# Windowed attention stream: keys, queries and values as one run at a slot's end, norms behind the products with V, the other engines reordered

## What is computed

```python
for i in range(DEPTH):
    x = attn_layer(shift_tokens(x), Wqkv[i], q_scale[i], k_scale[i], Wo[i]) + x
    x = ffn_layer(shift_tokens(x), ln_g[i], ln_b[i], W1[i], b1[i], W2[i], b2[i]) + x
```

## Time and profile before

| | us |
|---|---|
| median of three runs | 1957.38 |
| the profiled execution | 1957.33 |
| its span, first to last instruction | 1955.5 |
| TensorE busy | 1858.1 |
| VectorE busy | 1581.6 |
| ScalarE busy | 1405.1 |
| GpSimd busy | 1365.6 |

### The profile page before, as it was taken

The page is one execution under the profiler, slowest core; times in us unless marked ns, Lnnn a source line. Parts: engine busy times, 40 slices in busy tenths (PEclk is TensorE's granted clock), DMA queues, the critical chain, the costliest instruction groups (busy, mean ns, idle before and its releaser), DMA issues.

```text
span 1955.5 us, 68747 instructions
## 1 busy us (share of the span) xinstructions
PE 1858.1 (95%) x27097; PEld 1396.7 (71%) x27097; DVE 1581.6 (81%) x3046; ACT 1405.1 (72%) x2837; POOL 1365.6 (70%) x1442
## 2 busy tenths in 40 slices
PE   4999998899999999999999999999999999999998
PEld 3777766677777777777777777777777776777774
DVE  4677677898888888888888888888888888888876
ACT  2666665578777777777877777777777777777784
POOL 3000023798898787897878987878987879878780
PEclk9999999999999999999999999999999999999999
DMA  4000000344433334333334343443333343434332
GB/s 133 1 2 0 0 0 21 87 108 103 132 89 98 102 96 131 95 90 102 101 99 128 86 105 96 103 126 93 93 102 99 100 130 83 106 97 104 95 94 72
DMA packets 190582, 171.20 MB, mean 88 GB/s; under 512 B 32160, under 2 KB 186440, under 8 KB 190152
## 3 DMA queue, kind: packets, MB, share of 16 engines
q1 hardware_dynamic: 190280, 167.02, 32.6%
HBM read 21.14 MB, written 1.05 MB: 11 GB/s over the span
## 4 chain that ended last, share of the span: by engine, by line
PE 71%; ACT 12%; issue 7%; DVE 5%; POOL 2%; SPq 2%; DMA 1%; ACTq 0%; POOLq 0%; DVEq 0%
PE bank L896 7%; PE bank L934 7%; PE bank L864 7%; PE pair_bank L912 6%; PE bank L943 5%; PE bank L922 3%; PE bank L995 3%; PE bank L944 3%; PE bank L945 3%; PE bank L1017 3%; ACT sq L576 2%; PE bank L781 2%; PE bank L1009 2%; ACT probs L645 2%; PE pair_bank L903 2%
## 5 line engine op out<-in xcount | busy, mean ns | idle before, releaser
L415 POOL TENSOR_TENSOR z_raw<-rot_u,rot_v 128x256 f32<-128x256 f32 x768 | 553.6, 745 | 101.0 <-DVE rot_v L1210 94.4
L408 POOL TENSOR_TENSOR z_norm<-probs_t,z_raw 128x512 f32<-128x512 f32 x376 | 482.6, 1283 | 90.0 <-DVE probs_t L1289 87.3
L1209 DVE TENSOR_TENSOR rot_u<-bank,tabs 128x512 f32<-128x512 f32 x384 | 262.8, 684 | 166.6 <-ACT sq L576 166.3
L435 POOL TENSOR_TENSOR sqs<-sq 128x512 f32<-128x512 f32 x192 | 246.3, 1283 | 91.0 <-issue 90.8
L943 PE MATMUL bank<-x_high,w_high 128*128 128x256 f32 x768 | 301.4, 392 | 0.2 <-issue 0.2
L641 ACT ACTIVATE pair_bank<-pair_bank 128x512 f32<-128x512 f32 x192 | 111.7, 582 | 219.4 <-DVE pair_bank L1190 219.2
L576 ACT ACTIVATE sq<-bank 128x512 f32<-128x512 f32 x384 | 225.5, 589 | 49.6 <-PE bank L945 43.4
L1210 DVE TENSOR_TENSOR rot_v<-bank,tabs 128x512 f32<-128x512 f32 x384 | 261.0, 680 | 0.0
L934 PEld LDWEIGHTS bank<-probs_t,v_late 128*64 128x64 f32 x3072 | 155.0, 137 | 144.5 <-issue 144.5
L585 ACT ACTIVATE probs_t<-bank 64x512 f32<-64x512 f32 x384 | 226.8, 591 | 35.6 <-PE bank L922 33.3
L896 PE MATMUL bank<-sqs,consts 128*128 128x512 f32 x384 | 198.7, 599 | 25.2 <-POOL sqs L435 25.2
(11 more groups left out here) (186 smaller groups left out, 4545.7 us busy)
## 6 DMA issues: line engine op xcount, KB each, us to landing
zqk<-z_norm SPq DMA_DIRECT2D x1536, 64.0 KB, 2.1
v_late<-v_sb SPq DMA_DIRECT2D x192, 192.0 KB, 2.6
w_qkv<-in_L_ffn_Wqkv SPq DMA_DIRECT2D x18, 512.0 KB
v_late<-v_sb SPq DMA_DIRECT2D x192, 32.0 KB, 2.7
wo<-in_L_ffn_Wo SPq DMA_DIRECT2D x24, 128.0 KB, 2.4
w<-in_L_ffn_W SPq DMA_DIRECT2D x12, 170.5 KB, 2.9
consts<-in_constants SPq DMA_DIRECT2D x1, 1088.0 KB, 5.1
w_qkv<-in_L_attn_w_kv_up SPq DMA_DIRECT2D x2, 512.0 KB, 6.2
```

The costliest lines, as they stand in the source:

```text
L408: return pool.tensor_tensor(z_norm[:, parity, idx, :, :], rinv(m)[:, idx, :].unsqueeze(1).broadcast_to([P, 2, T]), z_raw[:, parity, idx, : ...
L415: a = pool.tensor_tensor(z_raw[:, parity, idx, half, :], rot_u[:, idx, half, :], rot_v[:, idx, 1 - half, :], ALU.add)
L1209: dve.tensor_tensor(rot_u[:, idx, :, :], src, tabs[:, 2 * idx, :, :], ALU.mult)
```

## The change

Only the order of steps within a slot moves, on four engines. The diff:

```diff
--- before.py
+++ after.py
@@ -420,8 +420,6 @@
                 if s == 0:
                     pool.wait_ge(S["pv_done"], STEPS)
                     pool.memset(spread[:, :, :, :], 0.0).then_inc(S["spread_zero"], 1)
-                if one:
-                    rotated(s + 4, s % 2, 1, "k_prod", "k_summed")
                 if two:
 
                     pool.wait_ge(S["bound_ready"], s + 4)
@@ -437,6 +435,7 @@
                     pool.wait_ge(S["q_summed"], s + 4)
                     normalise(s + 3, 0).then_inc(S["zn_ready"], 1)
                 if one:
+                    rotated(s + 4, s % 2, 1, "k_prod", "k_summed")
                     rotated(s + 4, s % 2, 0, "q_prod", "q_summed")
                 for g in range(G):
                     l = layer_begun(s, LAYER - 7 + g)
@@ -626,12 +625,12 @@
                 one, two = active(s, -4, GROUPS - 4), active(s, -3, GROUPS - 3)
                 three, four = active(s, 0, GROUPS), active(s, 1, GROUPS + 1)
                 normed = g == 0 and active(s, 2 * G, 2 * G + GROUPS)
-                if two and s >= 0:
-                    values_out(s + 3)
                 if s == 1:
                     act.wait_ge(S["spread_zero"], 2)
                 if four:
                     spread_out(s - 1)
+                if two and s >= 0:
+                    values_out(s + 3)
                 if mlp_slot(s, 17):
                     act.preload_act_table_set(LN_EXP)
                 if normed:
@@ -639,6 +638,8 @@
                 if three:
                     act.wait_ge(S["shifted"], s + 1)
                     act.activation(both, both, ACT.Exp).then_inc(S["raised"], 1)
+                if four:
+                    output_out(s - 1)
                 if two:
                     m = s + 3
                     act.wait_ge(S["n_done"], m + 1)
@@ -646,12 +647,6 @@
                     act.wait_ge(S["ln_done"], m + 1)
                     after(act, "zn_ready", m)
                     act.activation(rinv(m), ln_n(m), ACT.Exp, scale=-0.5).then_inc(S["rinv_ready"], 1)
-                if one:
-                    squares(s + 4, "k_prod", B_K, 1, "k_square")
-                l = layer_begun(s, LAYER - 5)
-                if l:
-                    rotary_scales(l)
-                    rotary_tables(l, 1)
                 l = layer_begun(s, LAYER - 4)
                 if l:
                     act.wait_ge(S["q_prod"], LAYER * l)
@@ -660,8 +655,6 @@
                     xc_squares((s - 7) // G)
                 if normed:
                     gained((s - 8) // G)
-                if four:
-                    output_out(s - 1)
                 for c in range(3):
                     if mlp_slot(s, 13 + c):
                         p = (s - 13 - c) // (2 * G)
@@ -673,8 +666,13 @@
                     gelus((s - 16) // (2 * G))
                 if one:
                     squares(s + 4, "lq_done", B_Q, 0, "q_square")
+                    squares(s + 4, "k_prod", B_K, 1, "k_square")
                 if session:
                     last_gelus((s - 16) // (2 * G))
+                l = layer_begun(s, LAYER - 5)
+                if l:
+                    rotary_scales(l)
+                    rotary_tables(l, 1)
                 l = layer_begun(s, LAYER + 6)
                 if l:
                     gains(l)
@@ -967,17 +965,15 @@
                     turn_windows(s - 1)
                 if active(s, 0, GROUPS):
                     windows(s, s // G, g)
-                if one:
-                    keys(s + 4)
                 if s == 0:
                     pe.wait_ge(S["yt_ready"], STEPS)
                     project_out(B_Y)
                 if active(s, 2, GROUPS + 2):
                     project_group(s - 2)
+                if four:
+                    weigh_windows(s - 1, (s - 1) // G, (s - 1) % G, (s - 1) // G % 2)
                 if two:
                     norms(s + 3)
-                if four:
-                    weigh_windows(s - 1, (s - 1) // G, (s - 1) % G, (s - 1) // G % 2)
                 for c in range(3):
                     if mlp_slot(s, 13 + c):
                         p = (s - 13 - c) // (2 * G)
@@ -1017,8 +1013,8 @@
                         mm = pe.matmul(B_M[:, :], w2[0:CW[c], c, :], hid[0:CW[c], c, :], start=(c == 0), stop=(c == 2))
                     mm.then_inc(S["mlp_done"], 1)
                 if one:
+                    keys(s + 4)
                     queries(s + 4)
-                if one:
                     values(s + 4, g, (s + 4) // G % 2)
                 if g == 2 and active(s, 6, 6 + GROUPS):
                     w, b = (s - 6) // G, (s - 6) // G % NB
@@ -1272,21 +1268,16 @@
             def slot(s):
                 g = s % G
                 one, two, three = active(s, -4, GROUPS - 4), active(s, -3, GROUPS - 3), active(s, 0, GROUPS)
+                if three:
+                    shift_windows(s)
                 if mlp_slot(s, 21):
                     mlp_residual((s - 21) // (2 * G), B_M)
                 if g == 3 and active(s, 7, 7 + GROUPS):
                     centred_out((s - 7) // G)
-                if three:
-                    shift_windows(s)
-                if one:
-                    rotate(s + 4, 1, B_K, "lk_done", "k_summed", "k_prod")
                 if g == 0 and active(s, 8, 8 + GROUPS):
                     normed_out((s - 8) // G)
                 if three:
                     weigh_down(s)
-                if two:
-                    dve.wait_ge(S["rinv_ready"], s + 4)
-                    dve.tensor_scalar(rinv(s + 3), rinv(s + 3), 1e12 / ROOT, None, ALU.min).then_inc(S["bound_ready"], 1)
                 if s == 0:
                     dve.wait_ge(S["wo_done"], NB + 1)
                     dve.tensor_copy(attn[:, NB - 1, :], B_Y[:, 0:T]).then_inc(S["res_done"], 1)
@@ -1301,7 +1292,11 @@
                     if mlp_slot(s, 17 + c):
                         p = (s - 17 - c) // (2 * G)
                         hidden_out(p, c, B_M, 2 * p + (2 if c == 2 else 1))
+                if two:
+                    dve.wait_ge(S["rinv_ready"], s + 4)
+                    dve.tensor_scalar(rinv(s + 3), rinv(s + 3), 1e12 / ROOT, None, ALU.min).then_inc(S["bound_ready"], 1)
                 if one:
+                    rotate(s + 4, 1, B_K, "lk_done", "k_summed", "k_prod")
                     rotate(s + 4, 0, B_Q, "q_square", "q_summed", "q_prod")
                 l = layer_begun(s, LAYER + 15)
                 if l:
```

## The result

| | us |
|---|---|
| before, median of 4 runs | 1957.74 (1956.3 to 1958.7) |
| after, median of 4 runs | 2005.41 (2003.48 to 2009.38) |
| ratio, with its 95% interval | 1.0254 (1.0240 to 1.0268) |
| profiled execution of after: time, span | 2005.69, 2003.9 |
| mean granted clock, before and after | 0.997, 0.987 |

A forecast was written before the change was run, and what follows sets the result against it. TensorE was taken as the bound. Seventeen plain periods at +0.80 (13.6), five split periods (+5.0), the first 16 slots (+1.9) and the causal part (0) gave +20.5 on 1957.3: 1978 us, range 1944 to 2000.

The forecast's parts named there:

- first 16 slots: Seven slots without MLP, centring or variance matmuls, each +0.38 for late spread copies less 0.11: +1.9 us in all.
- (b): ScalarE: keys' squares, now last before the next spread copies, wait for VectorE's rotation; its delay holds spread copies and TensorE.
- (c): VectorE: keys' rotation now stands behind softmax division, residual, MLP product and clipping; before, in the slot's first third.
- the wait in the second slot: Slot 81: TensorE's products with V wait 2.4 us for ScalarE's spread copies; slots 80-81 together +0.12.
- the new one in the third: Slot 82: products with V wait for spread copies held behind late keys' rotation and squares, +1.34 us.
- I take 0, because the kinds of matmul agree better: TensorE's output projection directly behind the scores: entry between 0 and 0.11 us, taken as 0.
- 6.66: Summed TensorE time in us of a slot after the change, with no projection entry; before, 6.77 without the wait.
- The rule weighed there: Weight loads overlap matmuls only where row groups differ, so TensorE's run order would not matter: saving 0.
- in slots 83-87 the rotation is early enough: VectorE's keys' rotation ends by 7.22 us in slots of 7.5 or more, so no wait there.
- Faster: Rival, chance 0.15: keys' squares in time in slot 82; a period -0.54, 22 times -12 us: 1945.
- much faster: Rival, chance 0.03: slot 81's wait goes as well, a further 53 us: near 1892.
- Slower still: Rival, chance 0.10: clipping meets GpSimd's rotation sums, half a us in four slots of eight, 44 us: 2015.

The follow-up runs named there:

- f2: Changed kernel with TensorE's norms back ahead of the products with V and ScalarE's copy of values ahead of the spread copies: 2036.36 us (1.0400).
- b1: Changed kernel with ScalarE's squares of the keys behind the next slot's spread copies, from slot 0 on: 2023.89 us (1.0335).
- b2: Changed kernel with VectorE's clip and keys' rotation ahead of the residual, MLP's product and input split in every slot: 2036.37 us (1.0412).
- b3: Changed kernel with VectorE's clip and keys' rotation ahead of the residual and MLP's product only in slots with s mod 4 = 1: 2003.95 us (1.0241).
- g1: Changed kernel with VectorE's MLP residual back ahead of the windows' maxima: 2012.89 us (1.0281).
- d1: Changed kernel with 20 spare mask matmuls ahead of the products with V in the second slot of a period: 2003.41 us (1.0240).
- c3: Kernel before with TensorE's keys moved behind the output projection: 1958.06 us (1.0008).
- e1: Kernel before, TensorE untouched, with the other engines' changed orders in causal slots only and ScalarE's output copy, queries' squares and last gelu moved: 1955.55 us (0.9994).
- e2: e1 with the weight conversions of split periods spread over slots 25, 27, 28 and 29 of 32: 1954.86 us (0.9994).
- f1: Changed kernel with TensorE's norms back ahead of the products with V, keys still at the end: 2087.14 us (1.0663).

## Why the prediction was right in sign and wrong in size

The spans differ by 48.4. By stretches of the two profiles:

| stretch | forecast | measured |
|---|---|---|
| up to slot 0 | 0 | -4.7 |
| first 16 slots | +1.9 | +4.4 |
| ordinary periods (17 counted, 16 full and a cut-off last) | +13.6 | +37.9 + 2.5 |
| five split periods | +5.0 | +8.3 |
| sum | +20.5 | +48.4 |

**Right.** The chain of (b) and (c) in all its links: the wait in the second slot (2.4; 2.34), the new one in the third (1.34; 1.29), the sums' and output copy's waits gone, the squares idle 2.04 for the rotation. f2, b1 and b2 each cut a link and the wait moved as the chain says. Slots 96 and 97 differ from the working by 0.28, and 0.22 of it is there when the logarithm starts (4.39 after the masks, 4.17 worked out); half of that is the entry of the next paragraph.

**Wrong: "I take 0, because the kinds of matmul agree better"** (the projection's entry behind the scores). It is 0.11, shown by 1.06 against 0.95 and by 0.97 against 0.86. This is the term that failed most: every slot of the working stood on 6.66 or had 0.11 taken off, and the plain slot measured 6.77, as before; measured less waits, a period went from 64.2 to 64.1. Counted in all eight slots, 0.88 over 22 periods is 19.4 us, with the first slots 21. That is the upper end: in the second and third slot of a period the entry runs out inside the wait for the spread copies, and six slots give 14.5. The text had this case: "at 0.11 the whole saving is gone", "17 to 20 more, 1997"; that leaves 8 us of the 2005, most of which the next paragraphs account for. The rule weighed there, of the Trainium skill (TensorE: Matmul & The Clock Gate, The mechanism), would have given the right saving, 0, though by a reason that the traces still do not bear out: matmuls with all 128 rows follow each other every 0.12 in the run of keys, while each takes 0.28.

**Wrong: "in slots 83-87 the rotation is early enough".** VectorE's residual of 1.50 in the sixth slot was not in the sum of steps. The seventh slot is 0.29 longer, 6.4 us over 22 periods. With the rotation earlier in the sixth slot the seventh is 8.06 (b3), with the residual ahead of the maxima it is 8.83 (g1).

**Missing: the clock.** The wait in the second slot was priced at its own length. It also took the granted clock down in 14 periods. Taking this away is worth 2.6 us over the 16 ordinary periods (35.3 in d1 against 37.9), since the third slot's wait hides behind it. With the longer split periods this is what hid the gain of b3.

**Mis-sized.** The first 16 slots wait 12 times and 9.3 us for the spread copies (slots 2 to 4 are 7.46, where before has 6.77); +0.38 had been worked out for seven of them, without the entry. The start came 4.7 us earlier: 2.2 of it by the causal slots' new order, which had been put at 0. The other 2.5 is no property of the change, but the granted clock in one stretch of the first 40 us, before (first line) and after (second):

```profile
31.50:38.70 7.20, 6.57 (x25) 5.25 (x26) 0.93 (x2) 1.67 (x3) 4.73 (x4) 0.53 0.18 42
31.50:38.70 7.20, 6.33 (x46) 5.64 (x47) 1.68 (x4) 2.97 (x5) 5.46 (x5) 1.00 0.08 11
```

At 0.53 TensorE does 25 matmuls in it, at 1.00 46, and the first causal scores start at 44.8 and at 42.2. b3 has 0.53 in this stretch and 44.8, g1 0.76 and 43.2, while c3 and e1, with the first steps of before, have 1.00 and start at 41.9 and 42.1. Without these 4.7 us, which the forecast did not have, the miss would have been 33 us and not 28: here luck made it smaller.

**Rivals.** Faster and much faster: out, the squares are never early. Slower still (2015), by the clip that meets GpSimd: the time came near it by another way. By its own term, 44 us on the forecast's 1978, it would have been 2022 and not 2015. The clip takes 536 ns on the mean of 188, where it took 554 before:

```profile
L1297 DVE TENSOR_SCALAR probs_t<-probs_t 128x512 f32<-128x512 f32 x188 | 100.8, 536 | 43.9 <-ACT probs_t L649 43.2
```

**Left open.** Of the 1.6 by which an ordinary period missed (+2.4, forecast +0.8), 0.66 to 0.88 is the entry (in six or in all eight slots), 0.29 the residual and 0.16 the clock (2.6 over 16 periods); the rest, 0.2 to 0.5, lies in steps of a tenth and was not taken apart, nor were the split periods' 3.3 beyond the forecast.

## What to carry to other kernels

The price of reordering matmuls belongs to pairs of neighbours: write down all the pairs of the old and of the new order and price each from a row, before a saving at one pair is counted. A wait that was taken away at one place came back at another (e1, e2, f2), in e1 where VectorE had no idle time for 11 us; so look first which engine has none in those slots. And such moves come as a set: TensorE's half alone cost eleven times, the other engines' half alone 2.5 times what both together cost.

## What the runs showed of the hardware

Behind a wait of 2.3 us, with full clock and no idle time before it, TensorE's granted clock fell in 14 of 22 periods; I had not expected so short a stop to matter. In f1 the wait was 3.15; the windows behind it:

```profile
1351.10:1354.50 3.40, 2.22 (x72) 1.46 (x70) 1.82 (x4) 3.39 (x5) 1.44 (x2) 1.00 0.34 83
...
1357.00:1360.00 3.00, 3.00 (x30) 1.52 (x30) 1.59 (x4) 1.30 (x2) 2.50 (x4) 0.50 0.27 67
1360.00:1363.00 3.00, 3.00 (x19) 1.92 (x16) 1.36 (x4) 1.80 (x3) 0.00 (x0) 0.65 0.31 74
```

```profile
1356.47 2.08 PE L894 MATMUL bank<-sqs,consts 128*128 128x512 f32 x2 [3.15 <-ACT v_sb L520]
```

0.50 of the clock is 1.2 GHz, the lower of its two levels: matmuls that TensorE was busy with took twice as long (2.08 against 1.13) for some 6 us after a stop of 3, and the slot is 13.66 where the same slot, with the clock kept, is 11.07. Yet the same kind of wait left the clock at 1.00 in 8 of the 22 periods of the changed kernel. What tells the two apart was not found.
